# A decoder layer on one Trainium2 core: the experts' rows in blocks of 512, 512 and 256 instead of 640 and 640

## The reference

```python
xr = x.reshape(S, d)                                  # 4096 rows of 512
probs = jax.nn.softmax(xr @ Wg, axis=-1)
gate_vals, expert_idx = jax.lax.top_k(probs, K)       # K = 2
...
dispatched = xr[dispatch_mask.reshape(-1) % S].reshape(E, C, d)   # E = 8, C = 1280
h = jax.nn.relu(jnp.einsum('ecd,edf->ecf', dispatched, w1))       # d = 512, f = 2048
expert_out = jnp.einsum('ecf,efd->ecd', h, w2)
...
out = jnp.einsum('ks,ksm->sm', combine_weights, rerouted)
```

## Time and profile before

| | us |
|---|---|
| median of 3 runs | 2927.71 |
| lowest, highest | 2920.79, 2928.13 |
| the profiled execution, its own time | 2925.62 |
| its span in the trace | 2923.9 |
| first product of the expert stage starts | 1091.07 |
| last matmul of the expert stage starts | 2910.06 |

### The profile page before, as it was taken

How to read it: one execution, slowest core, us unless ns; L and a number is a source line. 1 busy time by engine, 2 the same in 40 slices (tenths; PEclk the granted TensorE clock), 3 DMA queues, 4 the chain that set the end, 5 groups by cost and what they waited for, 6 DMA issues and landing times.

```text
span 2923.9 us, 45848 instructions
## 1 busy us (share of the span) xinstructions
PE 2794.9 (96%) x16150; PEld 2281.6 (78%) x16150; DVE 1237.2 (42%) x2155; ACT 878.7 (30%) x1700; POOL 842.0 (29%) x1306
## 2 busy tenths in 40 slices
PE   7979999988999939999999999999999999999998
PEld 6855555556666528999999999999999999999997
DVE  7757777646888823232232232132133133133111
ACT  2126666642656512221121121122122122122110
POOL 4546777631166640102101111012021021011010
PEclk9999999989999969999999999999999999999999
DMA  3102222242222223221122032032033033022110
GB/s 109 43 2 41 43 44 47 54 95 82 73 81 82 73 83 101 95 86 60 56 92 70 31 110 77 20 111 81 12 112 97 11 101 105 12 90 83 29 47 21
DMA packets 97510, 194.68 MB, mean 67 GB/s; under 512 B 22174, under 2 KB 23806, under 8 KB 97360
## 3 DMA queue, kind: packets, MB, share of 16 engines
q1 hardware_dynamic: 75504, 131.77, 15.3%
q0 software_dynamic: 21856, 60.73, 6.7%
HBM read 148.77 MB, written 38.94 MB: 64 GB/s over the span
## 4 chain that ended last, share of the span: by engine, by line
PE 62%; DMA 0%; POOL 0%; issue 0%; DVE 0%; DVEq 0%; ACT 0%; POOLq 0%
PE ex_hid L1826 31%; PE ex_acc L103 10%; PE ex_acc L102 10%; PE ex_acc L104 10%; PE ex_xb L1796 1%; DMA ex_ys<-xn_dram,ex_slot_gather 0%; POOL out_dram L1678 0%; DVE ex_ys L1739 0%; POOL ex_xg L1643 0%; POOL ex_ys L1658 0%; DMA ex_ys<-slot_table_dram 0%; PE ex_acc L1796 0%; DVE ex_xT0l L1722 0%; DVEq L72 0%; ACT ex_xT0h L1689 0%
## 5 line engine op out<-in xcount | busy, mean ns | idle before, releaser
L1747 DVE SCALAR_TENSOR_TENSOR ex_h0l<-ex_hid,ex_h0h 128x640 fp32r<-128x640 f32 x128 | 105.5, 824 | 681.9 <-ACT ex_h0h L1706 675.2
L1747 DVE SCALAR_TENSOR_TENSOR ex_h1l<-ex_hid,ex_h1h 128x640 fp32r<-128x640 f32 x128 | 105.4, 824 | 603.6 <-ACT ex_h1h L1706 546.2
L1706 ACT ACTIVATE ex_h0h<-ex_hid 128x640 fp32r<-128x640 f32 x128 | 90.2, 704 | 733.4 <-PE ex_hid L1826 733.4
L1706 ACT ACTIVATE ex_h1h<-ex_hid 128x640 fp32r<-128x640 f32 x128 | 90.2, 704 | 730.4 <-PE ex_hid L1826 693.0
L705 DVE TENSOR_REDUCE at_nb<-at_ring 128x2 f32<-128x512 f32 (+1 forms) x384 | 246.8, 686 | 120.5 <-PE at_ring L811 120.5
L1648 POOL COPY ex_gi<-ex_slot_gather 128x1 int32 (+1 forms) x82 | 15.3, 187 | 914.0 <-PE ex_xb L1796 909.2
L102 PE MATMUL ex_acc<-ex_w_h,ex_h1h 128*128 128x512 f32 x640 | 254.2, 397 | 0.0
L102 PE MATMUL ex_acc<-ex_w_h,ex_h0h 128*128 128x512 f32 x640 | 252.9, 395 | 0.0
L103 PE MATMUL ex_acc<-ex_w_l,ex_h1h 128*128 128x512 f32 x640 | 250.7, 392 | 0.0
L103 PE MATMUL ex_acc<-ex_w_l,ex_h0h 128*128 128x512 f32 x640 | 250.6, 392 | 0.0
L104 PE MATMUL ex_acc<-ex_w_h,ex_h1l 128*128 128x512 f32 x640 | 249.9, 391 | 0.0
(11 more groups left out here) (273 smaller groups left out, 5666.9 us busy)
## 6 DMA issues: line engine op xcount, KB each, us to landing
ex_raw<-in_w_tiles_dram SPq DMA_DIRECT2D x256, 256.0 KB
x_in<-in_x_dram SPq DMA_DIRECT2D x32, 256.0 KB
act<-at_raw SPq DMA_DIRECT2D x128, 64.0 KB
at_recb<-o_rec_dram SPq DMA_DIRECT2D x16, 512.0 KB
k<-in_x_dram SPq DMA_DIRECT2D x32, 256.0 KB, 2.6
cx_ctx<-in_ctx_dram SPq DMA_DIRECT2D x16, 512.0 KB
out_dram<-cx_res SPq DMA_DIRECT2D x16, 512.0 KB
xn_dram<-cx_prob SPq DMA_DIRECT2D x16, 512.0 KB
```

Source lines behind the costliest of these rows:

```text
L1706: act.activation(h[f % 2][0][:], hid[:, :, 0:HB], ACT.Relu).then_inc(sm["h_hi"], 1)
L1747: dve.scalar_tensor_tensor(h[f % 2][1][:], hid[:, :, 0:HB], 0.0, f32(h[f % 2][0][:]), ALU.max, ALU.subtract).then_inc(sm["h_lo"], 1)
```

## The change

`TILES = (4, 4, 2)`: an expert's rows are three blocks of 4, 4 and 2 tiles, the small one last.

- The first product of a slice is 4 parts x 3 passes over all the block's rows at once: 12 matmuls of 512 columns, or of 256 in the small block, through `split_passes`.
- `hid` is two tensors of one bank, used by turns with f. PE waits, before the first product of slice f, for the parts of slice f - 2.
- There are four `acc` banks, and `ys` holds four tiles. Seven banks are in use.
- `refilled` splits slices 0 to 13 of the next expert in steps 2 to 15 of the small block, and slices 14 and 15 in steps 4 and 5 of the next expert's first block. In the first expert four slices (`AHEAD`) are split before the loop, two of them behind the turned tiles; slices 4 to 15 follow in steps 0 to 11 of block 0.
- A block turns the tiles of the next one: 4 in steps 0, 3, 6, 9 of the first block, 2 in steps 0 and 3 of the second, 4 in steps 0, 3, 9 and 12 of the small one.
- The semaphore values, the gathers and the stores count by tiles, no longer by blocks of equal size.

The core of the diff:

```diff
-BLK = CAP // 2
-BT = BLK // P
+TILES = (4, 4, 2)
...
-        HB = BLK // 2
+        NB = len(TILES)
+        BASE = [sum(TILES[:b]) for b in range(NB + 1)]
+        WIDE, AHEAD = max(TILES), 4
...
-        hid = s.ps("ex_hid", [P, 2, 512])
-        acc = [s.ps(f"ex_acc{i}", [P, D]) for i in range(BT)]
+        hid = [s.ps(f"ex_hid{r}", [P, 512]) for r in range(2)]
+        acc = [s.ps(f"ex_acc{i}", [P, D]) for i in range(WIDE)]
...
-        TURN = {3 * i: i for i in range(BT)}
+        def turns(b):
+            n = TILES[(b + 1) % NB]
+            return {(0, 3, 9, 12)[i] if TILES[b] == 2 else 3 * i: i for i in range(n)}
...
-            if b == 0 and f + RW < NF and isinstance(e, int) and e == 0:
-                return 0, f + RW
-            if b == 1 and f >= 2 and not (isinstance(e, int) and e == E - 1):
+            fresh = isinstance(e, int) and e == 0
+            if b == 0 and fresh and f + AHEAD < NF:
+                return 0, f + AHEAD
+            if b == NB - 1 and f >= 2 and not (isinstance(e, int) and e == E - 1):
                 return e + 1, f - 2
-            if b == 0 and f < 2 and not (isinstance(e, int) and e == 0):
-                return e, NF - 2 + f
+            if b == 0 and 4 <= f < 6 and not fresh:
+                return e, NF - 6 + f
...
-                        pe.wait_ge(sm["h_lo"], ONE + NF * m + f)
+                        wait(pe, sm["h_lo"], NF * m + f - 1)
+                        out = hid[f % 2][:, 0:tiles * P]
                         for k in range(KD):
-                            for a, q in ((0, 0), (0, 1), (1, 0)):
-                                for z in range(2):
-                                    i = pe.matmul(hid[:, z, 0:HB], w1[a][:, f, k, :],
-                                                  xT[b][q][:, k, z * HB:(z + 1) * HB], start=k == 0 and a + q == 0,
-                                                  stop=k == KD - 1 and a == 1)
+                            q = split_passes(pe, out, [w[:, f, k, :] for w in w1], [x[:, k, :] for x in xT[b]],
+                                             k == 0, k == KD - 1)
```

More of the change, by code:

```diff
@@ L1673, in _ @@
                             .then_inc(rows_loaded, 16)
[L1674 to L1677, removed]
+                    for i in range(TILES[(b + 1) % NB]):
+                        gather(n + tiles + 2 + i, (BASE[b + 1] + i) % 2, False)
+                    for i in range(tiles):
+                        wait_apart(pool, sm["rows_done"], WIDE + n + i + 1, sm["passed_pool"])
                         pool.indirect_dma_start(io["out_rows"][:, :],
@@ L1695, in split_hi @@
                             e * (32 * NF // RW) + 32 * (f // RW + 1)))
-                wait(act, sm["used"], 2 * NF * e - NF + f + 1 if not isinstance(e, int) or e else 0)
+                wait(act, sm["used"], NB * NF * e - NF + f + 1 if not isinstance(e, int) or e else 0)
                 act.activation(w1[0][:, f, :, :].rearrange("p k n -> p (k n)"), raw[:, f % RW, 0, :], ACT.Copy)\
@@ L1771, in _, with turn @@
                 split_lo(0, f)
-            for i in range(BT):
-                turn_lo(0, 0, i)
+            for i in range(TILES[0]):
+                turn_lo(i, 0, i)
+            for f in range(RW, AHEAD):
+                split_lo(0, f)
             experts(dve, expert)
-            add_rows(2 * E - 1)
+            add_rows(NB * E - 1, ST - TILES[-1], TILES[-1])
         @block.tensor
         def _(pe):
-            def turn(m, i, parity, first):
-                n = BT * m + i
-                r = (parity * BT + i) % 2
+            def turn(e, c):
+                n, r = BASE[NB] * e + c, c % 2
                 source = xg[r]
-                if isinstance(n, int) and 2 <= n < BT:
+                if isinstance(n, int) and 2 <= n < TILES[0]:
                     source = ys[:, n, :]
                     pe.wait_ge(early[n - 2], 16)
-                elif isinstance(n, int):
-                    pe.wait_ge(gathered[r], 16 * (n // 2 + 1 - (early_of_ring[r] if n >= BT else 0)))
-                else:
-                    pe.wait_ge(gathered[r], first * (16 * BT) + 16 * ((parity * BT + i) // 2 + 1 - early_of_ring[r]))
-                bank = turning_bank(m, i)
+                elif isinstance(n, int) and n < 2:
+                    pe.wait_ge(gathered[r], 16)
+                else:
+                    pe.wait_ge(gathered[r], e * (8 * BASE[NB]) + 16 * (c // 2 + 1 - early_of_ring[r]))
+                bank = turning_bank(n)
                 if bank is xb:
@@ L1803, in _, with outputs @@
             pe.wait_ge(sm["slots_ready"], ONE + 1)
-            for i in range(BT):
-                turn(0, i, 0, 0)
-            def outputs(m, f):
+            for i in range(TILES[0]):
+                turn(0, i)
+            def outputs(e, b, f):
+                m, n = NB * e + b, BASE[NB] * e + BASE[b]
                 pe.wait_ge(sm["h_lo"], ONE + NF * m + f + 1)
-                for i in range(BT):
+                for i in range(TILES[b]):
                     if f == 0:
-                        pe.wait_ge(sm["rows_done"], ONE + BT * m + i + 1)
-                    hh, hl = (x[:].rearrange("p a n -> p (a n)")[:, i * P:(i + 1) * P] for x in h[f % 2])
+                        last = TILES[b - 1]
+                        done = 0 if isinstance(m, int) and m == 0 else n - last + min(i, last - 1) + 1
+                        pe.wait_ge(sm["rows_done"], ONE + WIDE + done)
+                    hh, hl = (x[:, i * P:(i + 1) * P] for x in h[f % 2])
                     q = split_passes(pe, acc[i][:], (hh, hl), [w[:, f, :] for w in w2], f == 0, f == NF - 1)
```

119 lines of the change are left out of this document (64 added, 55 removed).

## The result

| | before | after |
|---|---|---|
| median, us | 2926.93 (6 runs) | 2941.38 (6 runs) |
| lowest, highest | 2920.79, 2928.13 | 2939.82, 2950.76 |
| the profiled execution | 2925.62 | 2939.82 |
| its span | 2923.9 | 2938.1 |
| first product of the expert stage | 1091.07 | 1090.92 |

The ratio is 1.0058, with a 95% interval of 1.0047 to 1.0069. The forecast was 2909 us, 2901 to 2926.

What follows compares the result with a forecast made beforehand. PE, busy 96% of the span, was taken as the bound. Gains of 15.4 + 1.2 + 1.3 + 3.9 = 21.8 us less 3.5 gave 18.3: 2925.6 to 2907.3, plus 2.1 for the median: 2909 us, range 2901 to 2926.

Steps and rivals of the forecast that it cites:

- The matmul train: Expert stage's products: fewer, wider first-product matmuls take 6.91 us a slice instead of 7.04, 15.4 us less over 128 slices.
- rival 3: Passing from a 256-column to a 512-column matmul costs 0.09 us extra, 11.5 us in all: 2921 us; chance 0.09.
- rival 4: Fewer matmuls don't pay; only some 4 of the 15.4 us come: 2921 us; chance 0.05.
- The start: Before the stage's first products: one turned tile less saves 1.2 us, and the second first product's wait saves 1.3 us.
- The end: After the last matmul: the last block has two tiles, so three stores less, 3.9 us saved.
- What the small block must cover: Next expert's weight splits and loads under 2.80 us steps: buffer round 5.4 of 5.6 us; cost 3.5 us, bounds 0 and 53.
- the prediction's own sign of failure: Weight loads in the small blocks: the forecast fails if landings there pass 3.9 us on the mean.
- the formula: Small block's stall from landing L: about 6 x (L - 3.1) - 4.4 us a block, in seven blocks.
- rival 2: Weight transfers bind half way under the small block, L about 4.1, costing 11 us: 2917 us; chance 0.13.
- Rival 1: Weight transfers bind under the small block; at L = 4.6 they cost 32 us: 2938 us, slower; chance 0.12.
- the other waits of the small block: Its first step's relu low part, done at 4.1 us, wanted at 4.2: nothing counted, other bound 2.4 us.
- small blocks about 49.4 us long: Sign of being right: small blocks last this long in experts 0 to 6, and as long in expert 7.

Runs made afterwards that it cites:

- e8: The kernel before the change, with PE's loop over the experts written out; 2924.8 us.
- e3: The changed kernel with PE's loop over the experts written out, the other engines keeping their loops; 2916.0 us.
- e5: The changed kernel with four raw weight buffers instead of two, and `ex_filled` placed inside `ys` to make room; 2908.6 us.
- e9: The changed kernel with four raw weight buffers and PE's loop taking two experts a turn, so it goes back twice instead of five times; 2901.6 us.
- e1: The changed kernel with the small block in the middle, tiles (4, 2, 4); 2903.3 us.
- e4: The changed kernel without the weight loads for experts 1 to 7, splits and products kept, so the output is not the layer's; 2902.3 us.
- e6: The changed kernel with four raw weight buffers and PE's loop over the experts written out; 2895.9 us.

## Why the prediction was wrong

**The matmul train** was right in kind, and its term was too small. A wide first product and a wide second product, expert 3's block 0 (timeline of PE):

```profile
2069.09 0.39 PE L101 MATMUL ex_hid<-ex_xT0h,ex_w_h 128*128 128x512 f32 x1
...
2071.82 0.39 PE L101 MATMUL ex_acc<-ex_w_h,ex_h1h 128*128 128x512 f32 x1
...
2074.53 0.39 PE L101 MATMUL ex_hid<-ex_xT0h,ex_w_h 128*128 128x512 f32 x1
```

A step is 5.44 us (forecast 5.48); in the small block 12 of 256 columns take 1.43 us, as forecast. Three undisturbed blocks are 87.59 + 87.99 + 48.21 = 223.8 us, where two undisturbed ones of 640 rows take 2 x 113.35 = 226.7 (e8). That is 2.9 us an expert, 23 in all, against 15.4. The step that fell short is the rate from the earlier trace rows, 228.5 ns for 512 columns. There widths take turns. In the expert stage, too, the first five or six matmuls of 512 columns behind another width start 228 to 236 ns apart, and the further ones 226.7. The wide first products are 512 behind 512, which is worth 5 us; and the second products, which the sum left out, gain the other 3, since a slice changes width once and no longer twice. So rival 3 had a cost that exists, but at 0.03 us a passage and not 0.09, and before paid it too; rival 4 is out, fewer matmuls do pay. The Trainium skill's gap (TensorE: Matmul & The Clock Gate, "Back-to-back issue gap") is 2.5 ns above the columns; the section gives it for an isolated matmul. In this stream it is 13 ns, as before, and the gain was not the 3.8 us that the formula would have given.

**The start** was right. From SP's first load of the stage, the slot table, to the first product it took 15.7 us instead of 17.4 (1.7; forecast 1.64 for the tile), though the stage began 1.5 us later in this run. The second first product, which had waited 1.31 us, waits no more. Of 1.64 us for the tile the forecast had held back 0.4 for the low clock, and they were not lost: the clock was full from 1094 us on, 3.1 us behind the first product, where before it was low until 1095.8, for 4.7. That is luck: in e3 and e5, with the same start, it stayed low for 5.7 and 5.9 us.

```profile
1094.00:1096.00 2.00, 2.00 (x12) 1.65 (x11) 0.00 (x0) 0.60 (x2) 1.70 (x2) 1.00 0.84 274
```

**The end** gained 4.7 us (forecast 3.9): two stores where there were five, and 0.8 us less behind the last store.

```profile
2929.54 1.41 DVE L1750 SCALAR_TENSOR_TENSOR ex_ys<-ex_acc,ex_slot_gate,ex_ys 128x512 f32<-128x512 f32 x2 [2.03 <-PE ex_acc L103]
2931.22 1.02 POOL L1686 DMA_INDIRECT out_dram<-ex_ys,ex_rows_out  x1 [10.83 <-DVE ex_ys L1750]
2932.54 1.01 POOL L1686 DMA_INDIRECT out_dram<-ex_ys,ex_rows_out  x1 [0.30 <-issue]
```

**What the small block must cover** is the first step that failed, in its input more than in its formula. I took the landing L as the time to the end of the traffic, 2.9 us, and called the round 5.4 of 5.6 us: "so it just fits". The waiting split starts 0.5 us later, and the split stands 2.66 us before the issue on the mean, not 2.50, so a round alone on the queues is already 6.1. With others on them L is 4.18 us on the mean, not 3.4; the prediction's own sign of failure was 3.9. For the block shown above the formula gives 6 x (4.17 + 2.66 - 5.6) - 4.4 = 3.0 us. With e3's own mean of 4.07 it gives 2.4 us a block, 17 in all, where e3 measures 20.7; the forecast had 3.5. e3 ran at 2916 us, and rival 2 had "L about 4.1" and 2917. Its mechanism and its L are borne out, but that the times agree is luck: it had the stalls at 11 us instead of 20.7 and the gain at 21.8 instead of some 31. By the Trainium skill's HBM latency (DMA: Bandwidth & Descriptors, "Latency and other measured facts"), which the prediction set beside this, L would have been 4.9 and the time 2951; four of the twelve landings reach that, the mean does not. That the round barely fitted was a sign to give rivals 1 and 2 together more than 0.25.

**A way back in the loop had no term** at all. This is the second failed step, and the larger one: 17.3 us, and 6.5 of the clock. Rival 1 named 2938 us, but by landings of 4.6 us that did not occur on the mean; that the sum came near is chance. The trace of before could have told. One expert's end and the next one's start there, in PE's timeline:

```profile
1995.33 0.39 PE L102 MATMUL ex_acc<-ex_w_h,ex_h0h 128*128 128x512 f32 x1
...
1998.52 0.39 PE L104 MATMUL ex_acc<-ex_w_h,ex_h0l 128*128 128x512 f32 x1
1999.27 0.56 PE L1826 MATMUL ex_hid<-ex_xT0h,ex_w_h 128*128 128x320 f32 x2 [0.35 <-issue]
```

From the start of the last second product to the next expert's first product lie 3.94 us, 0.35 of them idle; this is one of the pieces in the earlier trace rows, which I passed over as nothing. At the five ways back the distance is 3.5 to 3.9 us, 3.7 on the mean, where 15 matmuls take 3.42: they covered it. In the small block only 6 are left, 1.39 us: 3.7 - 1.4 = 2.3 us bare, five times, so 12 us. In e9 the same distance is 3.76 us (3.09 the other time):

```profile
1764.59 0.40 PE L101 MATMUL ex_acc<-ex_w_h,ex_h0h 128*128 128x512 f32 x1
...
1765.75 0.39 PE L103 MATMUL ex_acc<-ex_w_h,ex_h0l 128*128 128x512 f32 x1
1768.35 0.49 PE L101 MATMUL ex_hid<-ex_xT0h,ex_w_h 128*128 128x512 f32 x1 [2.21 <-DVE ex_w_l L1742]
```

What fills it can be seen in the packets. At each of the 27 ways back in before, after, e1, e4, e5 and e9 one instruction block is loaded, in 0.9 to 1.5 us, and the next expert's first product starts 1.7 to 2.0 us after its end, every time. With PE's loop alone written out, such blocks still come, about every 25 us, but no first product comes late behind one. The instruction queue in the window 1996:1997 of before (packet from 1996.04 to 1997.51) and 1765:1766 of e9 (from 1765.15, for 1.43 us); nothing else of any size is moved in either:

```profile
q8 instruction: 1, 0.02, 9.2%
```
```profile
q8 instruction: 1, 0.02, 8.9%
```

So 2.7 to 3.2 us of the way back are the loading of PE's instructions at the loop's start and what follows it. That PE stands there for that block is read from these times; no run loads it sooner. What makes up the 1.8 us behind the block's end no run separates.

In the changed kernel the distance is 4.7 to 5.2 us (4.74 from 2239.03 to 2243.77), a microsecond more, although block and product stand as far apart there as elsewhere, 2.7 to 2.9 us. What is later is the block: it starts 2.0 to 2.5 us behind the start of the second product, in e5 and e9 0.2 to 0.7. PE had been standing for late low parts in these blocks, so the two causes add to each other; in e5, without late parts, the gaps are 9.7 us and not 16.5.

The two failed steps and the rest give the miss: 17.3 + 6.5 for the way back, 22.4 - 3.5 more for the stalls, less some 10 that the train, the start and the end gained over the forecast, are 33 us. The forecast was off by 32.

My claim that the other waits of the small block fit by 0.1 us held: e6's blocks show none. And "small blocks about 49.4 us long" counted one second product twice: 16 x 2.80, four turned tiles at 0.46 and 1.37 more for the wide block's last second product are 48.0; undisturbed they are 48.21.

## What to carry to other kernels

When work is moved under a shorter stretch, compare the round of each buffer with the stretch from waiter to waiter: to the start of the instruction that waited for the load, not to the end of its traffic; where the two are near each other, another buffer or an earlier release decides it. Ask also what the old length had hidden at loop ends: a few tenths of "issue" idle at each turn of a loop mean that its way back is as long as the work queued there, and shrinking that work lays it bare. The packets of the instruction queue show the way back by themselves. And a releaser that the profile names before a gap is only the last semaphore that rose; whether it is an operand tells if it can be the cause.

## What was not expected of the hardware

- PE's way back in a loop of some 1050 matmuls an expert: from the start of the last product before the branch to the first behind it 3.1 to 3.9 us in before, e5 and e9, 2.4 to 2.9 in e4, 4.7 to 5.2 in the changed kernel. In all 27 cases the first product starts 2.7 to 3.2 us after a 16 KB instruction block begins to load. Written out, the distance is the 1.39 us of the matmuls themselves.
- Gaps of 3 us in PE's work were followed by the lower clock level four times in five, at an average of 0.54 over 3.5 us (above). In e5, with gaps of 1.8 to 2.1 us, a stretch of 3.4 us at the lower level followed twice in five, in e9 behind gaps of 2.2 and 1.5 us it did not, nor behind the ten gaps of e1 and e4, up to 1.4 us. An example is this window of e5 right behind a gap, at 0.79 over 8 us:

```profile
1768.00:1776.00 8.00, 7.93 (x30) 6.33 (x31) 1.94 (x3) 1.12 (x2) 0.00 (x0) 0.79 0.01 2
```

- Loads slow down for more than bytes. A 256 KB pair that lands in 3.4 us alone takes 4.9 with one 16 KB instruction block beside it (84 loads, above). In the middle of such a landing nearly all of the DMA engines are idle:

```profile
2238.00:2239.00 1.00, 0.01 (x1) 0.00 (x0) 0.98 (x3) 0.00 (x0) 0.00 (x0) 1.00 0.06 8
```
